# Who normalises the router's features, and in which order the vector engine works, in a fused graph and attention network

## The chip, the cores and the metric

The kernel runs on one core of a Trainium2 chip. The metric is the device time of one execution in microseconds (us), the median of several runs. Besides, one execution of the kernel is profiled, and everything below that is read from a trace is read from that one.

## The reference

Two layers, each with a graph part, a mixing part and a feed-forward part, over 1250 nodes of 512 values. What matters here is the end of the last layer: the graph part ends in a batch norm and a ReLU and is added to `x`; then `x` is layer-normalised and goes through a routed feed-forward net in which each of 32 experts takes its 39 best rows.

```python
h = h @ W2 + b2
h = jax.nn.relu(batch_norm(h, g2, be2))                 # end of the graph part
...
xf = _layernorm(x).reshape(bs, H)                       # (x - m) / sqrt(v + 1e-5), by row: the router's features
h = xf @ W_router + b_router
Sm = jax.nn.softmax(h, axis=-1)
G_ek, idx_ek = jax.lax.top_k(Sm.T, k)                   # 39 rows for each of 32 experts
tokens = xf[idx_ek]
up = jnp.einsum('gjkh,ghf->gjkf', tok_g, W_up) + b_up
act = jax.nn.silu(up)
Eout = jnp.einsum('ekf,efh->ekh', act, W_down) + b_down
y = zeros.at[idx_ek.reshape(-1)].add(G_ek * Eout)
x = x + y
```

## The kernel before, in words

The program is written for each engine by hand, with semaphores between them; every engine does its instructions in the order in which they stand. The 1250 rows are ten tiles of 125 rows (`TOK`), and the tiles form three groups (`GROUPS`): tiles 0 to 3, 4 to 7, and 8 and 9. The names that the change and the prediction's steps touch, in the order of the work:

- ScalarE applies batch norm and ReLU to the hidden values `H2T`, which lie with features on the partitions (L1050). TensorE turns them tile by tile with transposes (`gin_t`, L1606 to L1612, four transposes a tile) into one of two PSUM row banks, and the vector engine adds a tile from PSUM to `X` (L2211). `open_row` lets TensorE write a row bank only once the entry two before has been drained, so TensorE can be two tiles ahead of the vector engine at most.
- Layer norm of `X`: `stats` (L1717, L1720) takes mean and variance of the tiles of a group on the vector engine; GpSimd's `rstd` (L643, L645) makes 1/sqrt(variance + eps) of them with a power; `normalise` on the vector engine (L1725) writes `XF`, the router's features, and counts each tile on `ln_out`.
- `turn_rows("moe_t")` (L1137): TensorE waits until all ten tiles have been added to `X` (the row banks are then free), and for each group until its tiles of `XF` are there; it turns each group in four row entries, one for each 128 features, twelve entries in all. ScalarE drains each entry to `XFT` (`drain_turned`, L850).
- The gate: TensorE multiplies `XFT` with the router's weights (L1620), the vector engine adds the bias, a softmax follows (L2217 to L2225), and five rounds of top-8 search (L2235 to L2238) give the rows of each expert.
- SyncE stores `X` to the output and `XF` to DRAM (`xf_dram`, L458); GpSimd gathers the chosen rows from there (L804) once the search is done and both stores have landed. Then eight groups of four experts: products with `w_up` (L1676) and `w_down` (L1696), whose weights SyncE streams in from DRAM through a ring of buffers (L454), and a scatter into the output.
- `unread_products(n, entry)` (L1084 to L1088) is a helper on TensorE: n products of the identity with a constant, 256 columns wide, into a column bank of PSUM whose content nobody reads. It is used during the search and before the first gathered rows.

The order of the vector engine in the stretch around the change is this piece of code:

```python
for g, (lo, hi) in enumerate(GROUPS):
    for t in range(lo, hi):
        o = filled(ROW["gin_t"] + t)
        dve.tensor_tensor(X[:, t], o[0:TOK, :], X[:, t], ALU.add).then_inc(rows_free, 1)
    if g:
        normalise("moe", g - 1, X, XF)
    stats("moe", g, X, lambda t: dve.wait_ge(rows_free, ROW["gin_t"] + t + 1))
normalise("moe", 2, X, XF)
```

An earlier layer norm of the same kernel ("ffn") already has two of its groups normalised by ScalarE (L927), with a bias of -mean/std that GpSimd makes in two more instructions (L704, L705).

Of the kernel before, what the change touches and what calls it, by code (L numbers as in the profile page):

```python
# [5 lines left out]
ALU = mybir.AluOpType  # L6
ACT = mybir.ActivationFunctionType
# [16 lines left out]
GROUPS = [(0, 4), (4, 8), (8, 10)]  # L24
# [34 lines left out]
LN_EPS = 1e-5  # L59
# [99 lines left out]
def build(nc, a, out):  # L159
    with ExitStack() as ctx:  # L160
# [87 lines left out]
        X = rows(0)  # L248
# [367 lines left out]
        def _(pool):  # L616
# [29 lines left out]

            for g, (lo, hi) in enumerate(GROUPS):
# [49 lines left out]
            for g in range(2):  # L697
                lo, hi = GROUPS[g]
                rstd("sage", g)
                pool.wait_ge(ln_mv, LN_TILES["ffn", g])  # L700
                pool.tensor_scalar(ln_rs[:, lo:hi], ln_mv_t[:, lo:hi, 1], LN_EPS, None, ALU.add).then_inc(ln_eps, 1)
                pool.wait_ge(ln_eps, LN_NUMBER["ffn", g] + 1)
                done(pool.tensor_tensor(ln_rs[:, lo:hi], ln_rs[:, lo:hi], minus_half[:, lo:hi], ALU.pow))
                done(pool.tensor_tensor(ln_nm[:, lo:hi], ln_mv_t[:, lo:hi, 0], ln_rs[:, lo:hi], ALU.mult))  # L704
                pool.tensor_scalar(ln_nm[:, lo:hi], ln_nm[:, lo:hi], -1.0, None, ALU.mult).then_inc(ln_rstd, 1)  # L705
# [80 lines left out]
            for g in range(3):  # L786
                rstd("moe", g)
# [43 lines left out]
        def _(act):  # L831
# [8 lines left out]
            def drain_turned(stage, dst, affine=None):  # L840

                n = ROW[stage]
                for g, (lo, hi) in enumerate(GROUPS):
                    for c in range(C):
# [78 lines left out]
            def normalise_ffn(g):  # L923

                act.wait_ge(ln_rstd, LN_NUMBER["ffn", g] + 1)
                for t in range(*GROUPS[g]):
                    act.activation(XL[:, t], X[:, t], ACT.Identity, scale=ln_rs[:, t:t + 1],  # L927
                                   bias=ln_nm[:, t:t + 1]).then_inc(ln_out, 1)

# [13 lines left out]
            normalise_ffn(0)  # L943
# [4 lines left out]
            normalise_ffn(1)  # L948
# [102 lines left out]
            drain_turned("moe_t", XFT)  # L1051
# [19 lines left out]
        def _(pe):  # L1071
# [534 lines left out]
            for t in range(TILES):  # L1606
                if t in (0, 4, 8):
                    pe.wait_ge(bn2_relu, t + 4)
# [4 lines left out]

            turn_rows("moe_t", XF, "moe")
# [89 lines left out]
        def _(dve):  # L1704
# [503 lines left out]
            for g, (lo, hi) in enumerate(GROUPS):  # L2208
# [3 lines left out]
                if g:  # L2212
                    normalise("moe", g - 1, X, XF)
                stats("moe", g, X, lambda t: dve.wait_ge(rows_free, ROW["gin_t"] + t + 1))
            normalise("moe", 2, X, XF)
# [118 lines left out]
```

## Time and profile before

| | us |
|---|---|
| median of 3 runs | 1571.0 |
| lowest and highest run | 1566.73 and 1575.32 |
| the profiled execution, its time | 1569.41 |
| the profiled execution, its span (first to last instruction) | 1567.6 |

| engine | busy us | share of the span |
|---|---|---|
| TensorE matmul | 1431.1 | 91% |
| TensorE weight load | 957.2 | 61% |
| VectorE | 669.5 | 43% |
| GpSimd | 434.9 | 28% |
| ScalarE | 391.3 | 25% |

The span ends 1.8 us before the time does; both are of the same execution. The mean granted clock of TensorE is 0.969 of full speed. In the chain of work that ended last TensorE holds 78%, the vector engine 9% and DMA 7%. A share is an average over stages, so what one edit is worth is read in the stage that it touches, here the stretch from 1219 to 1244 us.

### The profile page before, as it was taken

Reading aid. Unit: us, or ns where it says so; the run is one execution under the profiler, and the core shown is the slowest. Engines: PE = TensorE matmul, PEld = TensorE weight load, DVE = VectorE, ACT = ScalarE, POOL = GpSimd, SP = SyncE. Lnnn points to the kernel's source line nnn. Section 1 sums busy time; section 2 is a strip of 40 time slices with the busy share of each in tenths; the row PEclk is TensorE's granted clock in tenths of the full one; section 3 lists DMA queues with packets and bytes.
Section 4 is the critical chain, followed back from the end, with each engine's and each line's share of the span. In section 5 each row is a group of like instructions: output and inputs, shape, how many; then the busy total and the mean of one; then the engine's idle time right before and its main releaser. Section 6 shows DMA issues by size and latency. Waiting matters only on the chain.

```text
span 1567.6 us, 18598 instructions
## 1 busy us (share of the span) xinstructions
PE 1431.1 (91%) x7122; PEld 957.2 (61%) x7122; DVE 669.5 (43%) x1252; ACT 391.3 (25%) x648; POOL 434.9 (28%) x432
## 2 busy tenths in 40 slices
PE   4999987999999799999999979999998689998996
PEld 2546744544777687666666635778866475554553
DVE  6522036789665424566666240624252651100100
ACT  2210002221412432544444324111151301000010
POOL 2300013002020310788888628002010112222111
PEclk9999998999999799999999999999999899999999
DMA  8000010031200230111110091012001949999995
GB/s 270 23 0 0 1 55 1 1 104 41 86 1 0 88 106 1 54 32 42 26 26 9 16 202 47 0 33 102 1 1 61 408 162 343 383 396 396 411 411 222
DMA packets 43789, 178.88 MB, mean 114 GB/s; under 512 B 6086, under 2 KB 6672, under 8 KB 41781
## 3 DMA queue, kind: packets, MB, share of 16 engines
q1 hardware_dynamic: 40141, 171.87, 30.7%
q0 software_dynamic: 3248, 5.48, 1.6%
q8 instruction: 57, 0.93, 0.2%
q10 hardware_dynamic: 313, 0.35, 0.1%
q14 instruction: 30, 0.25, 0.0%
HBM read 153.46 MB, written 21.66 MB: 112 GB/s over the span
## 4 chain that ended last, share of the span: by engine, by line
PE 78%; DVE 9%; DMA 7%; ACT 2%; issue 2%; POOL 1%; SPq 1%; DVEq 0%; POOLq 0%; ACTq 0%
PE psum L1696 9%; PE psum L1105 8%; PE psum L1096 7%; PE psum L1446 6%; PE psum L1676 5%; PE psum L1127 4%; PE psum L1432 3%; PE psum L1292 3%; PE psum L1537 3%; DMA arena<-in_w_down 3%; DMA arena<-in_w_in 3%; PE psum L1434 3%; PE psum L1246 2%; PE psum L1255 2%; PE psum L1310 2%; PE psum L1599 2%
## 5 line engine op out<-in xcount | busy, mean ns | idle before, releaser
L739 POOL TENSOR_TENSOR arena<-arena 125x420 f32<-125x420 f32 x192 | 178.3, 929 | 27.1
L1696 PE MATMUL psum<-arena 128*39 128x512 f32 (+1 forms) x704 | 157.4, 603 | 15.1 <-DMA arena<-in_w_down 8.8
L2044 DVE TENSOR_REDUCE neg_max<-psum 125x1 fp32r<-125x1250 f32 x80 | 116.8, 1460 | 100.9 <-PE psum L1400 53.2
L1004 ACT ACTIVATE arena<-psum 125x420 f32<-125x420 f32 x240 | 107.5, 521 | 124.1 <-PE psum L1434 124.1
L1696 PEld LDWEIGHTS psum<-arena 128*39 128x39 f32 (+1 forms) x704 | 51.7, 117 | 115.1 <-issue 108.2
L1096 PE MATMUL psum<-arena 128*128 128x512 f32 (+1 forms) x288 | 104.2, 523 | 6.1 <-DMA arena<-in_w_in 5.4
L824 POOL DMA_INDIRECT out_x<-arena,idx x32 | 44.9, 1402 | 209.4 <-DMA out_x<-arena,idx 118.3
L1446 PE MATMUL psum<-arena 125*64 125x210 f32 x960 | 102.7, 349 | 0.0
L1676 PEld LDWEIGHTS psum<-arena 128*128 128x128 f32 (+1 forms) x704 | 93.3, 187 | 8.0 <-issue 7.3
L1676 PE MATMUL psum<-arena 128*128 128x156 f32 (+1 forms) x704 | 95.4, 297 | 1.9 <-DMA arena<-in_w_up 1.4
L2269 DVE TENSOR_SCALAR arena<-psum,gates 39x512 f32<-39x512 f32 x32 | 24.0, 749 | 166.9 <-PE psum L1696 166.6
L1432 PE MATMUL psum<-arena_r 128*125 128x420 f32 x240 | 92.5, 386 | 0.7 <-ACT arena_r L993 0.7
L1096 PEld LDWEIGHTS psum<-arena 128*128 128x128 f32 x288 | 55.2, 193 | 55.0 <-issue 49.3
L1434 PE MATMUL psum<-arena_r 128*125 128x420 f32 (+1 forms) x240 | 84.9, 354 | 0.0
L1065 ACT ACTIVATE arena<-psum,vec 128x156 f32<-128x156 f32 (+1 forms) x88 | 28.2, 388 | 220.5 <-PE psum L1676 220.4
L1446 PEld LDWEIGHTS psum<-arena 125*64 125x64 f32 x960 | 61.9, 136 | 30.5 <-ACT arena L1004 16.0
L1865 DVE TENSOR_SCALAR arena<-arena,edge_key 125x500 bf16<-125x500 f16 x200 | 69.4, 347 | 25.0 <-PE psum L1230 23.9
L1127 PE MATMUL psum<-arena 128*125 128x512 f32 (+3 forms) x264 | 72.2, 433 | 1.7 <-ACT arena L873 1.3
L1137 PE MATMUL psum<-ident,arena 125*128 125x125 f32 x160 | 32.9, 356 | 34.7 <-DVE arena L1725 20.9
L671 POOL TENSOR_TENSOR arena<-arena 125x512 f32<-125x512 f32 x10 | 13.1, 1311 | 183.2 <-DVE arena L1847 183.2
L1127 PEld LDWEIGHTS psum<-arena 125*128 125x128 f32 (+2 forms) x264 | 43.4, 190 | 28.3 <-issue 23.2
L1432 PEld LDWEIGHTS psum<-arena_r 128*125 128x125 f32 x240 | 44.5, 186 | 24.7 <-issue 22.9
(407 smaller groups left out, 2451.7 us busy)
## 6 DMA issues: line engine op xcount, KB each, us to landing
arena<-in_w_down SPq DMA_DIRECT2D x96, 768.0 KB, 19.2
arena<-in_w_up SPq DMA_DIRECT2D x32, 682.5 KB, 19.4
arena<-in_w_down SPq DMA_DIRECT2D x32, 512.0 KB, 19.7
adj<-a_spill SPq DMA_DIRECT2D x1, 5468.8 KB
bc<-k_dram SPq DMA_DIRECT2D x16, 312.5 KB, 4.3
gw<-in_gw SPq DMA_DIRECT2D x2, 2048.0 KB, 9.3
arena<-in_wkqv SPq DMA_DIRECT2D x1, 3072.0 KB, 19.9
a_spill<-adj SPq DMA_DIRECT2D x1, 2843.8 KB
```

Of the source, the lines that this page charges most:

```text
L739: pool.tensor_tensor(SUMS[rnd % 2], SUMS[rnd % 2], PT[s % P_RING], ALU.add).then_inc(sum_added, 1)
L1004: act.activation(PT[s % P_RING], ring(step_entry(s))[:, 0:QW], ACT.Exp).then_inc(ring_done, 1)
L1096: ins = pe.matmul(o[0:w, lo:hi], lhs(c, m), rhs(c)[:, lo:hi], start=c == 0, stop=c == k - 1)
L1105: ins = pe.matmul(o[:, lo:hi], lhs[a_part][:, c, m * 128:m * 128 + 128], rhs[b_part][:, c, lo:hi], start=i == 0 and c == 0, stop=i == 2 an ...
L1127: ins = pe.matmul(o[0:p, 0:w], lhs(c, t), rhs(c, t), start=c == 0, stop=c == k - 1)
L1432: pe.matmul(o, KHH[h % 3][:, tok(t)], QS[:, h, q0:q1], start=True, stop=False)
L1434: pe.matmul(o, KLO[h % 2][rows_used, tok(t)], QM[h % 2][rows_used, q0:q1], start=False, stop=True).then_inc(ring_full, 1)
L1446: ins = pe.matmul(av_bank[rnd % 2][64 * i:64 * i + 64], VA[:, t, h * DK:h * DK + DK], PT[s % P_RING][:, i * QH:i * QH + QH], start=t == 0, ...
L1676: ins = pe.matmul(o[0:w, (f - 3 * q) * 512:(f - 3 * q) * 512 + 4 * CAP], UPQ[(4 * g + c) % 6][:, f * 128:f * 128 + w], TKT[g % 2][:, c], s ...
L1696: ins = pe.matmul(o[64 * j:64 * j + CAP, :], ACTT[g % 2][0:w, f, at:at + CAP], DN[e % 5][0:w, f], start=f == 0, stop=f == FT - 1)
L1865: dve.tensor_scalar(win_hot[s], win_iota, float(WIN_COLS * w), edge_key_all[:, bass.ds(tile, 1)], ALU.add, ALU.is_equal)
L2044: dve.tensor_reduce(neg_max[:, k:k + 1], max_bank[:, 0:N], AX.X, ALU.max, negate=True).then_inc(max_ready, 1)
```

## The change

Three things. The first group of `XF` is normalised by ScalarE (`normalise` in its block, called before it drains the first `moe_t` entry), and GpSimd makes the bias for it (`rstd_mean`, the code that "ffn" already used, now a function). The vector engine no longer normalises between its groups: it adds and takes the statistics of all three groups first and normalises groups 1 and 2 at the end. And TensorE gets four unread products before tile 4 of `gin_t` and six before `moe_t`.

```diff
+            def rstd_mean(name, g):
+
+                k, (lo, hi) = LN_NUMBER[name, g], GROUPS[g]
+                pool.wait_ge(ln_mv, LN_TILES[name, g])
+                pool.tensor_scalar(ln_rs[:, lo:hi], ln_mv_t[:, lo:hi, 1], LN_EPS, None, ALU.add).then_inc(ln_eps, 1)
+                pool.wait_ge(ln_eps, k + 1)
+                done(pool.tensor_tensor(ln_rs[:, lo:hi], ln_rs[:, lo:hi], minus_half[:, lo:hi], ALU.pow))
+                done(pool.tensor_tensor(ln_nm[:, lo:hi], ln_mv_t[:, lo:hi, 0], ln_rs[:, lo:hi], ALU.mult))
+                pool.tensor_scalar(ln_nm[:, lo:hi], ln_nm[:, lo:hi], -1.0, None, ALU.mult).then_inc(ln_rstd, 1)
...
-            for g in range(3):
-                rstd("moe", g)
+            rstd_mean("moe", 0)
+            rstd("moe", 1)
+            rstd("moe", 2)
...
-            def drain_turned(stage, dst, affine=None):
+            def normalise(name, g, src, dst):
+
+                act.wait_ge(ln_rstd, LN_NUMBER[name, g] + 1)
+                for t in range(*GROUPS[g]):
+                    act.activation(dst[:, t], src[:, t], ACT.Identity, scale=ln_rs[:, t:t + 1],
+                                   bias=ln_nm[:, t:t + 1]).then_inc(ln_out, 1)
+
+            def drain_turned(stage, dst, affine=None, ahead=None):
 
                 n = ROW[stage]
                 for g, (lo, hi) in enumerate(GROUPS):
+                    if ahead and g == 0:
+                        ahead(g)
...
-            drain_turned("moe_t", XFT)
+            drain_turned("moe_t", XFT, ahead=lambda g: normalise("moe", g, X, XF))
...
             for t in range(TILES):
                 if t in (0, 4, 8):
+                    if t == 4:
+                        unread_products(4, COL["up"])
                     pe.wait_ge(bn2_relu, t + 4)
...
+            unread_products(6, COL["up"])
             turn_rows("moe_t", XF, "moe")
...
                     dve.tensor_tensor(X[:, t], o[0:TOK, :], X[:, t], ALU.add).then_inc(rows_free, 1)
-                if g:
-                    normalise("moe", g - 1, X, XF)
                 stats("moe", g, X, lambda t: dve.wait_ge(rows_free, ROW["gin_t"] + t + 1))
+            dve.wait_ge(ln_out, LN_OUT["moe"] + GROUPS[0][1])
+            normalise("moe", 1, X, XF)
             normalise("moe", 2, X, XF)
```

The rest of the diff puts "ffn" on the same two functions, with the same instructions in the same order.

On the vector engine, from the first adds of the graph part to the gate, the order before (L2211 adds a tile, L1717 and L1720 are the statistics, L1725 normalises, L2217 is the gate's bias):

```order
L2211 TENSOR_TENSOR arena<-psum,arena 125x512 x4
L1717 BN_STATS ln_st<-arena 125x6 x4
L1720 BN_AGGR ln_mv_t<-ln_st 125x2 x4
L2211 TENSOR_TENSOR arena<-psum,arena 125x512 x4
L1725 TENSOR_SCALAR arena<-arena,ln_mv_t,ln_rs 125x512 x4
L1717 BN_STATS ln_st<-arena 125x6 x4
L1720 BN_AGGR ln_mv_t<-ln_st 125x2 x4
L2211 TENSOR_TENSOR arena<-psum,arena 125x512 x2
L1725 TENSOR_SCALAR arena<-arena,ln_mv_t,ln_rs 125x512 x4
L1717 BN_STATS ln_st<-arena 125x6 x2
L1720 BN_AGGR ln_mv_t<-ln_st 125x2 x2
L1725 TENSOR_SCALAR arena<-arena,ln_mv_t,ln_rs 125x512 x2
```

And in the changed kernel, where the same lines are ten further down:

```order
L2221 TENSOR_TENSOR arena<-psum,arena 125x512 x4
L1727 BN_STATS ln_st<-arena 125x6 x4
L1730 BN_AGGR ln_mv_t<-ln_st 125x2 x4
L2221 TENSOR_TENSOR arena<-psum,arena 125x512 x4
L1727 BN_STATS ln_st<-arena 125x6 x4
L1730 BN_AGGR ln_mv_t<-ln_st 125x2 x4
L2221 TENSOR_TENSOR arena<-psum,arena 125x512 x2
L1727 BN_STATS ln_st<-arena 125x6 x2
L1730 BN_AGGR ln_mv_t<-ln_st 125x2 x2
L1735 TENSOR_SCALAR arena<-arena,ln_mv_t,ln_rs 125x512 x6
```

Four of the ten normalising instructions have gone to ScalarE, and the six that are left stand behind the last add, which TensorE's `moe_t` waits for, instead of in front of it (four before stood ahead of that add).

On TensorE, the changed kernel between the last product of the graph part (L1587) and the gate (L1630); L1620 turns `gin_t`, L1144 turns `moe_t`, L1095 are the unread products:

```order
L1587 MATMUL psum<-k_sq,arena 125x512 x10
L1620 MATMUL psum<-ident,arena 125x128 x16
L1095 MATMUL psum<-neg_half,ident 128x256 x4
L1620 MATMUL psum<-ident,arena 125x128 x24
L1095 MATMUL psum<-neg_half,ident 128x256 x6
L1144 MATMUL psum<-ident,arena 128x125 x40
L1630 MATMUL psum<-arena,neg_half 32x315 x16
```

Before, the two rows of L1095 are not there, and the 40 transposes of `gin_t` stand in one piece.

## Rows read from the trace of the kernel before

**Rows 1.** The chain that ended last, 1190 to 1567 us: start us, us, what.

```profile
1219.94 0.72 PE psum L1611 x4
...
1222.85 2.38 DVE ln_st L1717 x4
1225.23 0.28 DVE ln_mv_t L1720 x4
1225.51 0.59 DVE arena L2211
...
1226.14 2.08 PE psum L1611 x8
...
1228.25 0.69 DVE arena L2211
1228.94 1.82 DVE arena L1725 x4
1230.76 2.38 DVE ln_st L1717 x4
1233.14 0.28 DVE ln_mv_t L1720 x4
1233.42 1.18 DVE arena L2211 x2
...
1241.39 0.60 ACT arena L850
...
1243.40 0.39 ACT arena L850
```

**Rows 2.** Busy time of each engine in stretches of the expert stage.

```profile
core 0: us, PE busy (x) PEld busy (x) DVE busy (x) ACT busy (x) POOL busy (x), PEclk, DMA share, GB/s
1283.00:1294.80 11.80, 11.80 (x90) 11.80 (x91) 0.00 (x0) 4.15 (x10) 1.54 (x2) 1.00 0.13 39
...
1310.00:1540.00 230.00, 213.84 (x1234) 127.63 (x1232) 24.72 (x38) 24.71 (x77) 45.79 (x35) 0.98 1.02 401
```

**Rows 3.** TensorE in order of time, 1219 to 1244 us.

```profile
1219.94 3.67 PE L1611 MATMUL psum<-ident,arena 128*125 128x128 f32 x20 [0.35 <-DVE arena L2181]
1226.14 3.81 PE L1611 MATMUL psum<-ident,arena 128*125 128x128 f32 x16 [2.53 <-DVE arena L2211]
1234.65 7.20 PE L1137 MATMUL psum<-ident,arena 125*128 125x125 f32 x34 [4.70 <-DVE arena L2211]
```

**Rows 4.** Busy time in single microseconds; columns as in the stretches above.

```profile
1225.00:1226.00 1.00, 0.00 (x0) 0.00 (x0) 1.00 (x7) 0.00 (x0) 0.32 (x2) 1.00 1.02 412
...
1228.00:1229.00 1.00, 0.98 (x5) 0.80 (x4) 0.84 (x3) 0.00 (x0) 0.00 (x0) 0.50 1.02 418
...
1230.00:1231.00 1.00, 0.00 (x0) 0.00 (x0) 1.00 (x3) 0.00 (x0) 0.00 (x0) 1.00 1.02 418
...
1236.00:1237.00 1.00, 1.00 (x6) 0.77 (x5) 1.00 (x3) 0.76 (x2) 0.00 (x0) 0.50 1.02 420
...
1240.00:1241.00 1.00, 0.97 (x8) 0.72 (x8) 0.37 (x1) 0.88 (x2) 0.00 (x0) 1.00 1.01 411
```

**Rows 5.** ScalarE in order of time, the drains of `moe_t`.

```profile
1235.78 0.59 ACT L850 ACTIVATE arena<-psum 128x500 f32<-128x500 f32 x1 [15.05 <-PE psum L1137]
1236.61 0.59 ACT L850 ACTIVATE arena<-psum 128x500 f32<-128x500 f32 x1 [0.24 <-PE psum L1137]
...
1239.38 2.88 ACT L850 ACTIVATE arena<-psum 128x500 f32<-128x500 f32 x5 [0.41 <-PE psum L1137]
```

**Rows 6.** ScalarE and GpSimd in order of time around 476 us, the "ffn" norm.

```profile
474.70 1.03 POOL L703 TENSOR_TENSOR ln_rs<-ln_rs,minus_half 125x4 f32<-125x4 f32 x1
...
476.38 2.94 ACT L927 ACTIVATE arena<-arena,ln_nm,ln_rs 125x512 f32<-125x512 f32 x4 [0.26 <-POOL ln_nm L705]
```

**Rows 7.** GpSimd in order of time, 1225 to 1235 us.

```profile
1225.91 1.04 POOL L645 TENSOR_TENSOR ln_rs<-ln_rs,minus_half 125x4 f32<-125x4 f32 x1
```

**Rows 8.** TensorE in order of time, one round of seven unread products (two records each).

```profile
1262.75 3.29 PE L1088 MATMUL psum<-neg_half,ident 128*128 128x256 f32 x14 [1.28 <-DVE arena L2238]
```

**Rows 9.** The vector engine in order of time, statistics of the last group.

```profile
1236.72 1.28 DVE L1717 BATCH_NORM_STATS2 ln_st<-arena 125x6 f32<-125x512 f32 x2
1237.92 0.30 DVE L1720 BATCH_NORM_AGGREGATE ln_mv_t<-ln_st 125x2 f32<-125x6 f32 x2
```

**Rows 10.** SyncE and GpSimd in order of time: next weights after the stores, first gather.

```profile
1266.09 1.30 SPq L454 DMA_DIRECT2D arena<-in_w_down  x3
1277.31 1.09 POOL L804 DMA_INDIRECT arena<-xf_dram,pair_idx  x1 [29.86 <-DVE pair_idx L2245]
```

More of the change, by code:

```diff
@@ L697, in _ @@
             for g in range(2):
-                lo, hi = GROUPS[g]
                 rstd("sage", g)
[L700 to L705, printed above, removed]
+                rstd_mean("ffn", g)
             rstd("sage", 2)
@@ L921, in high_sums @@
                 act.activation(AGG_PARTS[g][0][:, m, 0:w], agg_bank(k)[:, 0:w], ACT.Copy).then_inc(agg_hi, 1)
[L923 to L928, printed above, removed]
             def drain_ffn(g):
@@ L942, in _ @@
                 high_sums(1, m)
-            normalise_ffn(0)
+            normalise("ffn", 0, X, XL)
             high_sums(1, C - 1)
@@ L947, in _ @@
                 high_sums(2, m)
-            normalise_ffn(1)
+            normalise("ffn", 1, X, XL)
             drain_ffn(1)
```

## The prediction

> **What bounds the kernel now.** I first read the chain of work that ended last, because the change sits in a stretch of 25 us and only what lies on this chain counts. From 1222.85 us on the chain stays on the vector engine: statistics of group 0, adds, the four normalising instructions of group 0 (1.82 us), statistics of group 1 (2.38 and 0.28), and the two last adds (1.18), which end at 1234.60 [rows 1]. It leaves the engine only once, for 2.08 us, to wait for TensorE's turns of tiles 6 and 7. TensorE begins to turn the router's features at 1234.65, after 4.70 us without work [rows 3], and the last drain ends at 1243.40 + 0.39 = 1243.79 [rows 1].
>
> Next I read the expert stage, to see whether time saved here arrives at the end. Until 1294.8 TensorE does the first group's up products with hardly any DMA beside it (39 GB/s); from 1310 to 1540 the DMA share is 1.02 at 401 GB/s [rows 2]. So the end is set by a stream of weights that runs at the rate of the DMA engines. Most of it cannot start before the first group's up products have freed buffers, and those hang on the routing. A routing that ends x us earlier moves the start of the stream and with it the end by x.
>
> Last, the granted clock. It is 1.00 at 1225, 0.50 at 1228, 1.00 again at 1230, 0.50 at 1236 and 1.00 at 1240 [rows 4]: each fall to the half level (1.2 GHz) came after one of TensorE's two pauses, 2.53 and 4.70 us long [rows 3], each rise to 2.4 GHz came while or after TensorE turned tiles. These are the two waits that the change fills.
>
> **The change part by part.** 1. *Normalising group 0 leaves the vector engine's chain:* -1.82 us [rows 1].
>
> 2. *The same work on ScalarE.* GpSimd starts its power for group 0 at 1225.91 [rows 7]. In the "ffn" norm, which has the same instructions, ScalarE starts 476.38 - 474.70 = 1.68 us after the power's start and takes 2.94 us for four tiles [rows 6]. That gives 1225.91 + 1.68 + 2.94 = 1230.5 us. ScalarE has nothing else to do then: it sat idle for 15.05 us before its first drain [rows 5]. The features of group 0 are wanted when the last add is done, by the sum below at 1232.1, so the part is free with 1.6 us to spare. The two extra GpSimd instructions for the bias cost nothing either: the next group's statistics come some 5 us later. If that cover were gone, the cost would be what is left of the 2.94 us. Here a rule stands against the change. The trace has four tiles in 1.82 us on the vector engine and in 2.94 us on ScalarE [rows 1, 6]. The Trainium skill (ScalarE: Activation LUTs, Rules for kernel authors) says that multiplying and adding belong on VectorE and not on ScalarE. The trace agrees in kind, with 1.6 times for float32; by the rule alone the sum would be 1.1 us worse. I don't charge it, since the slower engine has the slack.
>
> 3. *Four unread products before tile 4.* Seven took 3.29 us at full clock [rows 8], 0.47 each, so four take 1.9. Tile 3's is the third of the turns that begin at 1219.94 [rows 3], so it ends near 1219.94 + 3 x 0.72 = 1222.1, the four end near 1224.0 and the turn of tile 4 (0.72 us for four transposes and the way to the vector engine, [rows 1]) near 1224.8. The vector engine asks for it at 1225.51 [rows 1]. Free, with 0.7 us to spare. TensorE's pause shrinks from 2.53 us to about 1.
>
> 4. *Tiles 6 and 7 turned at full clock.* Before, two turns cost 2.08 us at half clock, against 0.72 each [rows 1]. From 1226.14 the add of tile 6 starts at 1226.86 and that of tile 7 at 1227.58, where it started at 1228.25: -0.67 us. Bounds: 0 if the clock falls all the same, -0.67 if it does not. I take -0.67, as the pause that is left is far shorter than both after which the clock fell.
>
> With 1 and 4 the last add ends at 1234.60 - 1.82 - 0.67 = 1232.1.
>
> 5. *Six unread products before the features' turns:* 6 x 0.47 = 2.8 us. Tile 7's add ends at 1228.27 and frees the bank for tile 9, whose turn ends near 1229.0, so they end at 1231.8, before 1232.1. Free at full clock, but with only 0.3 us to spare; this is the tightest cover of the change. At half clock they take about 5.6 us, and then they stand in the way (rival 2).
>
> 6. *The late normalising of groups 1 and 2.* Four features' entries of group 0 are turned at once from 1232.1. Group 1 waits for the vector engine: statistics of group 2 take 1237.92 + 0.30 - 1236.72 = 1.50 us [rows 9], then normalising group 1 takes 1.82, so 1232.1 + 1.50 + 1.82 = 1235.4. This new wait takes the place of the old one. Group 0's four entries, drained at 2.88 / 5 = 0.58 us each [rows 5], are done at about the same time, so the loss by it is under 1 us. Group 2 follows about 1 us later, and is in time.
>
> 7. *The turns at full clock.* First drain of group 1 at 1235.4 + 0.72 = 1236.1 us, four drains at 0.60: 1238.5. From the end of group 1's last drain to the end of all took 1243.79 - (1241.39 + 0.60) = 1.80 us before, already at full clock [rows 1]. So the drains end at 1240.3, against 1243.79: **-3.5 us**. At half clock the drains came every 0.83 us [rows 5]. The bounds of this part are -1.8 (only the normalising goes) and -3.5. I take -3.4, near the far end, since rounding leaves 0.1.
>
> 8. *What comes after.* The gate, the softmax and the search keep their order and only start earlier. The stores: SyncE was held until the store of the features had landed and issued the next weights at 1266.09; the first gather started at 1277.31 [rows 10]. The gather waits for those stores too. With the routing 3.4 us earlier it starts at 1273.9, still 7.8 us behind the landing. So the gain passes.
>
> The profiled execution took 1569.41 us; the sum gives 1569.4 - 3.4 = 1566.0. It stands 1.6 us under the median of the runs shown, so on the median's scale the forecast is 1571.0 - 3.4 = **1567.6 us**, or -0.2%. That is below 0.5% (7.9 us), which is about what a measurement of this kernel can tell from no change.
>
> **The rivals.** *Rival 1, the clock falls all the same.* The products shorten the pauses but the half level still comes for one of the two stretches. For it: the level fell at about 1226.5, after TensorE had been busy until 1223.6 and had just begun again [rows 3, 4], so it lags what the engine does. Against it: the stretch from 1226 to 1232 is now nearly full. The result is -1.8, the normalising alone: 1569.2 us. The Trainium skill (TensorE: Matmul & The Clock Gate, What's actually happening) says that the number of slow matmuls at a start differs from run to run, which would make this rival come in some executions and not in others.
>
> *Rival 2, slower: the six products block the turns.* If the clock is at the half level when tile 9's turn ends, then near 1229.9 as before, the six end at 1229.9 + 5.6 = 1235.5, 0.9 us after TensorE starts on the features now. If the turns then run at the old pace, the result is +0.9: 1571.9 us. It decides from 0.79 us a product on ((1234.65 - 1229.9) / 6), against 0.47 at full clock. Against it: the clock had risen by 1230 even in the kernel before [rows 4].
>
> *Rival 3, the gain gets lost on the way.* The end is set by a stream of weights, and part of it is issued on the landing of the stores (1266.09), which does not move because the DMA engines are already full while `gin_t` and `moe_t` run (share 1.01 to 1.02, [rows 4]). If the first group's start hung on that, the result would be 1571.0 us, no change. Against it: 11 us between the landing and the gather [rows 10], and the DMA engines are nearly idle just before 1294.8 [rows 2].
>
> *Rival 4, more than forecast.* The stream of weights falls in a slightly better place. It lasts 230 us at 401 GB/s [rows 2]; 1% more rate is 2.3 us on top of the forecast: 1565.3 us. Nothing in the change makes it so.
>
> **How the numbers follow.** Forecast 0.55, rival 1 0.22, rival 2 0.07, rival 3 0.08, rival 4 0.08. All cases lie between 1565.3 and 1571.9. The three runs before lie up to 4.3 us from their median, and the median of the new ones may be off by a good part of that; so the range reaches some 3 us below the lowest case and 1.5 us above the highest: 1562.5 to 1573.5. Faster by over 0.5% means under 1563.1, which no case gives, only a case with the spread on top: 0.11. Slower by over 0.5% needs over 1578.9, 7 us above the worst case: 0.03. Within 0.5%: 0.86.
>
> **What the new profile would show.** ScalarE's four normalising instructions start near 1227.6 and end near 1230.5. TensorE's first feature turn starts near 1232.1, preceded by a pause under 1 us, and there is a short pause before group 1's turns, ended by the vector engine. The granted clock is 1.00 from 1219 to 1240 (rival 1: 0.50 somewhere in it; rival 2: 0.50 near 1230, and unread products that end after 1234). The last drain ends near 1240.3, the first gather starts near 1273.9, the next weights are issued near 1266 as now. The time from the first gather to the end stays as it is; if it grows by what the routing saved, rival 3 holds. I would be wrong if the vector engine waited for ScalarE's tiles, or if the turns waited for the unread products.

## The result and the profile after

| | before | after |
|---|---|---|
| median of 12 runs each, us | 1570.78 (1565.49 to 1575.32) | 1566.14 (1564.85 to 1569.07) |
| ratio | | 0.9975, interval 0.9963 to 0.9987 |
| profiled execution, us | 1569.41 | 1565.74 |
| its span, us | 1567.6 | 1563.8 |

The changed kernel is 3.9 us faster by the ratio (2.0 to 5.8 by its interval); the two medians themselves lie 4.6 us apart. The 3.9 us are a quarter of a per cent, inside the half per cent called "same" ahead of the result, and the 1566.1 us lie 1.5 us under the forecast of 1567.6.

The earlier stages do not start at the same microsecond in two traces, so everything below is counted from an **anchor**, the end of the last add of the graph part ahead of `gin_t` (1219.89 in the kernel before, 1218.88 in the changed one). The change's stretch ends with the last drain of `moe_t`: 23.90 us behind the anchor before (1243.79), now 1238.79 + 0.39 - 1218.88 = 20.30.

The chain that ended last, of the changed kernel (start us, us, what), answers to [rows 1]:

```profile
1221.85 2.38 DVE ln_st L1727 x4
1224.23 0.28 DVE ln_mv_t L1730 x4
1224.51 0.59 DVE arena L2221
...
1225.88 1.29 DVE arena L2221 x2
1227.17 2.38 DVE ln_st L1727 x4
1229.55 0.28 DVE ln_mv_t L1730 x4
1229.83 1.17 DVE arena L2221 x2
1231.00 1.19 DVE ln_st L1727 x2
...
1232.33 1.91 DVE arena L1735 x4
...
1234.29 0.66 PE psum L1144 x4
...
1238.79 0.39 ACT arena L864
```

Between the statistics of group 0 and those of group 1 the four normalising instructions are gone. They now stand behind the last add (1231.00), and the chain runs through them there: the new wait of the prediction's step 6.

ScalarE in order of time, of the changed kernel, answers to [rows 5, 6]:

```profile
1226.59 2.93 ACT L849 ACTIVATE arena<-arena,ln_nm,ln_rs 125x512 f32<-125x512 f32 x4 [8.55 <-POOL ln_nm L655]
```

The four tiles are ready at 1229.52. Nobody wants them before the last add, 1231.00, so 1.5 us are spare.

TensorE in order of time, of the changed kernel, answers to [rows 3]; the bracket is the idle time ahead of the group and what ended it:

```profile
1220.96 1.89 PE L1095 MATMUL psum<-neg_half,ident 128*128 128x256 f32 x8
...
1225.14 1.30 PE L1620 MATMUL psum<-ident,arena 128*125 128x128 f32 x8 [1.42 <-DVE arena L2221]
...
1227.77 2.76 PE L1095 MATMUL psum<-neg_half,ident 128*128 128x256 f32 x12
...
1231.06 1.07 PE L1144 MATMUL psum<-ident,arena 125*128 125x125 f32 x8 [0.54 <-DVE arena L2221]
...
1234.29 1.07 PE L1144 MATMUL psum<-ident,arena 125*128 125x125 f32 x8 [0.77 <-DVE arena L1735]
```

The pauses of 2.53 and 4.70 us have become 1.42, 0.54 and 0.77 us. An unread product has two records here and a transpose one, so `x8` is four products of L1095, but eight transposes. The whole stretch ran at the full level, as its busy times show (columns as in [rows 2]; the 1.00 behind the counts is the granted clock):

```profile
1216.00:1246.00 30.00, 21.38 (x141) 14.93 (x139) 20.25 (x44) 11.28 (x22) 5.33 (x11) 1.00 1.02 415
```

The span is 3.8 us shorter. In pieces: the stages ahead ended 2.7 us earlier, the piece just ahead of the anchor took 1.7 us more, the change's stretch 3.6 us less, the routing 0.3 us less, and the time from the first gather to the end 1.1 us more. Only the third of these five is the change's own; experiments had to say what the others are. The 0.3 us of the routing (last drain to first gather) come and go with the execution: it took 33.2 us in five of the fourteen traces below and 33.5 us in nine, and after_b, the changed kernel again, has 33.5.

### The profile page after: what moved, and what is told of

It reads as the page before. It is cut to its first block, busy times and chain, and to the rows that moved or that the text cites. A ratio compares the mean times of both kernels' runs of the same rounds, so it can differ in the third digit from the quotient of the medians.

```text
span 1563.8 us, 18641 instructions
## 1 busy us (share of the span) xinstructions
PE 1433.6 (92%) x7142; PEld 956.9 (61%) x7142; DVE 667.6 (43%) x1248; ACT 393.4 (25%) x652; POOL 436.5 (28%) x434
## 4 chain that ended last, share of the span: by engine, by line
PE 75%; DVE 9%; DMA 8%; SPq 3%; issue 2%; ACT 2%; POOL 1%; DVEq 0%; POOLq 0%; ACTq 0%
PE psum L1112 8%; PE psum L1706 7%; PE psum L1103 7%; PE psum L1453 6%; PE psum L1134 4%; DMA arena<-in_w_down 4%; PE psum L1686 4%; PE psum L1439 3%; PE psum L1299 3%; PE psum L1544 3%; DMA arena<-in_w_in 3%; PE psum L1441 3%; SPq L454 3%; PE psum L1253 2%; PE psum L1262 2%; PE psum L1317 2%
## 5 line engine op out<-in xcount | busy, mean ns | idle before, releaser
L1144 PE MATMUL psum<-ident,arena 125*128 125x125 f32 x160 | 28.9, 320 | 32.1 <-DVE arena L1735 22.0
```

## The experiments

There are five measures. **Ahead** is the time from ScalarE's last drain of `gin2`, the stage ahead, to the anchor. **Last add**, **first drain** and **last drain** are `gin_t`'s last add and `moe_t`'s drains, counted from the anchor. **Rest** runs from the first gather to the end. All in us, from one trace each.

| kernel | ahead | last add | first drain | last drain | rest |
|---|---|---|---|---|---|
| before | 11.07 | 14.71 | 15.9 | 23.90 | 290.3 |
| after | 12.77 | 12.12 | 12.86 | 20.30 | 291.4 |
| before_b | 14.08 | 14.18 | 15.38 | 22.83 | 291.3 |
| after_b | 11.07 | 12.13 | 12.87 | 20.29 | 293.4 |
| no_unread | 11.08 | 12.62 | 13.37 | 21.22 | 290.4 |
| unread_only | 11.07 | 13.94 | 14.68 | 21.80 | 292.0 |
| all_vector | 11.07 | 12.11 | 16.08 | 24.15 | 290.5 |
| twelve | 11.07 | 12.12 | 14.69 | 21.60 | 290.9 |
| double_scalar | 11.07 | 12.11 | 14.35 | 21.26 | 290.7 |
| down4_late | 14.04 | 12.12 | 12.85 | 20.27 | 290.7 |
| after_b2 | 14.09 | 12.11 | 12.85 | 20.28 | 291.1 |
| no_unread2 | 11.08 | 12.63 | 13.37 | 21.20 | 290.3 |
| best | 11.07 | 12.11 | 12.86 | 20.28 | 290.1 |
| g1_first | 14.08 | 12.12 | 12.86 | 20.05 | 290.9 |

All of them share one small edit in an early stage, so before_b is the kernel before with that edit, and after_b and after_b2 are the changed kernel with it. It adds a constant to both sides of a wait against a number, so that the number stays positive, and bounds the number where it is loaded:

```diff
-            done(dve.tensor_tensor(rng[:, 7], rng[:, 3], rng[:, 1], ALU.subtract))
+            done(dve.scalar_tensor_tensor(rng[:, 7], rng[:, 3], float(TILE_CODE // BODY), rng[:, 1], ALU.add, ALU.subtract))
...
-                dve.memset(small[0:1, 28 + s:29 + s], 0.0).then_inc(hot_free[s], BODY)
+                dve.memset(small[0:1, 28 + s:29 + s], 0.0).then_inc(hot_free[s], BODY + TILE_CODE)
...
-                turn = dve.value_load(ranges[0:1, 2 * WINDOWS + w:2 * WINDOWS + w + 1])
+                turn = dve.value_load(ranges[0:1, 2 * WINDOWS + w:2 * WINDOWS + w + 1], min_val=0, max_val=4 * TILE_CODE)
```

### The two kernels with that edit

> The kernel before, with one early edit that all my kernels share: the number that the vector engine waits against in the edge loop is kept positive (a constant 256 is added on both sides, one extra bound on the load). It touches nothing after 400 us. Measures, also for all later runs: A = from the end of the last drain of gin2 on ScalarE to the end of the last slice_o add; R = from there to the end of the last moe_t drain; G = from there to the first gather; S = from there to the end of the span. In the trace of before A is 11.1, R 23.9, G 33.5, S 290.3 us. Expected: the same within 0.3 us for R and G, 1566 to 1575 us in all. Rival: the edit costs time of its own: over 3 us more, all of it before 400 us.

Measured: 1573.36 us, ratio to before 1.0013 (0.9997 to 1.0029). The edit costs nothing that this can tell. The last drain came at 22.83, 1.1 us earlier than in the first trace of before, though nothing of this stretch was edited: the kernel before has a spread here of its own, since it depends on where the clock falls and rises. In the first trace 5.1 us of the `moe_t` turns ran at the half level (from 1234.65 to about 1239.7), in before_b 3.2 us (from 1237.85 to about 1241.0). Against the mean of the two, 23.4, the change is worth 3.1 us, not 3.6.

> The changed kernel with the same early edit. R was 20.3 us in the trace of after (R 3.6 shorter than before), A 12.8, G 33.2, S 291.4. Theory (the gain is made between the last slice add and the last drain, by 1.8 us of normalising off the vector engine's chain and the rest by a clock that stays at full level): R 20.3, time 3 to 5 us under before_b. Rival (a part of the gain of the medians is made elsewhere, or is spread of the runs): R 20.3 but under 2 us of difference in the times.

Measured: 1567.98 us, 0.9987 (0.9971 to 1.0003); last drain 20.29, the same as in the changed kernel to 0.01 us. The median lies 5.4 us under before_b's, where 3 to 5 us were expected, while against the kernel before the interval still includes no change; the times scatter by more than the stretch gives. The rest grew to 293.4 us, which is the subject of down4_late.

### Without the unread products, and the products alone

The edit of no_unread against the changed kernel; unread_only puts the same lines into the kernel before:

```diff
-                    if t == 4:
-                        unread_products(4, COL["up"])
...
-            unread_products(6, COL["up"])
```

> The changed kernel without its ten unread products; ScalarE's part and the new order stay. Theory (reordering and clock add up): the last add comes 1.8 us earlier than before, the clock falls to the half level in one of TensorE's waits, the drains come every 0.83 us: R 22.1, granted clock 0.50 in some microseconds between 1224 and 1240, time 1.5 to 2 us above after_b. Rival (the shorter waits of the new order keep the clock up without products): R 20.3 to 20.6, clock 1.00 throughout, time as after_b.

> The kernel before with the ten unread products alone; normalising and order as before. Theory: tiles 6 and 7 are turned at full clock (-0.67 us), the turns of moe_t begin 0.7 us earlier and run at full clock until group 2, which waits for the vector engine: R 22.4, time 1 to 2 us under before_b. Rival (the drains follow the clock alone, the vector engine is no limit): R 21.0. Second rival (the clock falls all the same, since the pause before moe_t is still 2 us): R 23.2 or more.

Without the products (no_unread) the last drain came at 21.22, not at about 22.1 as expected, and 1565.64 us, 0.9970 (0.9955 to 0.9985). With the products alone on the old order (unread_only) it came at 21.80, where 22.4 was expected, and 1569.37 us, 0.9986 (0.9971 to 1.0001). The times went other ways than expected: no_unread lay 2.3 us under after_b and not 1.5 to 2 us above it, and unread_only 4.0 us under before_b and not 1 to 2 us, so what follows is read from the traces. The new order, with ScalarE's part in it, is worth more, and the products less, than I had charged: on top of the new order the ten products save 21.2 - 20.3 = 0.9 us. On the old order they save between 1.0 us (22.83 - 21.80) and 2.1 us (23.90 - 21.80), depending on which trace of before one takes.

That the products do work through the clock is seen in TensorE's order of time without them, here from the repeat no_unread2:

```profile
1224.58 3.86 PE L1618 MATMUL psum<-ident,arena 128*125 128x128 f32 x16 [2.53 <-DVE arena L2218]
...
1231.01 4.71 PE L1144 MATMUL psum<-ident,arena 125*128 125x125 f32 x24 [2.57 <-DVE arena L2218]
```

and in its single microseconds:

```profile
1225.00:1226.00 1.00, 1.00 (x7) 1.00 (x6) 0.55 (x2) 0.00 (x0) 0.82 (x3) 0.50 1.06 434
...
1229.00:1230.00 1.00, 0.00 (x0) 0.00 (x0) 1.00 (x6) 0.00 (x0) 0.14 (x1) 1.00 1.06 436
...
1232.00:1233.00 1.00, 0.98 (x5) 0.67 (x4) 1.00 (x5) 0.86 (x2) 0.47 (x2) 0.50 1.02 405
```

The pauses of 2.53 and 2.57 us are each followed by a fall to 1.2 GHz. But the falls are short and cost 0.5 us at the last add (12.62 against 12.12) and 0.4 us behind it. The reason for the small price lies in the order itself: group 1 is not ready before the vector engine has normalised it, and slow turns of group 0 run in that wait. In the row above TensorE turns group 0 and half of group 1 in one piece of 24, where the changed kernel waits 0.77 us ahead of group 1.

In unread_only the pause ahead of `moe_t` is still 2.36 us:

```profile
1233.56 1.07 PE L1137 MATMUL psum<-ident,arena 125*128 125x125 f32 x8 [2.36 <-DVE arena L2214]
```

Eight transposes in 1.07 us is the pace at the full level, the same as in the changed kernel. A pause of that length did not bring the half level here.

### ScalarE's part taken back

```diff
-            rstd_mean("moe", 0)
+            rstd("moe", 0)
...
-            drain_turned("moe_t", XFT, ahead=lambda g: normalise("moe", g, X, XF))
+            drain_turned("moe_t", XFT)
...
-            dve.wait_ge(ln_out, LN_OUT["moe"] + GROUPS[0][1])
+            normalise("moe", 0, X, XF)
```

> The changed kernel, but group 0 is normalised by the vector engine too, behind the last add (GpSimd then makes no bias for it). Theory: the last add is where it was (12.1 us after the last slice add), and the turns of moe_t wait for group 0, ready at 12.1 + 1.5 (statistics of group 2) + 1.8 = 15.4, so the first drain starts at 16.1, the rest follows at 0.58 us an entry and R is 22.7, against 20.3. So ScalarE's part is worth 2.4 us once the order is changed. Rival (ScalarE's part only frees the engine of 1.8 us): R 22.1. Rival (the order alone is the change): R 20.5.

A single run, 1570.32 us beside 1570.07 for before; last drain 24.15, where 22.7 was expected and the changed kernel has 20.3. TensorE in order of time of all_vector:

```profile
1235.77 1.04 PE L1144 MATMUL psum<-ident,arena 125*128 125x125 f32 x8 [3.79 <-DVE arena L1735]
...
1237.06 5.41 PE L1144 MATMUL psum<-ident,arena 125*128 125x125 f32 x26 [0.25 <-ACT arena L864]
```

All ten normalising instructions now stand behind the last add, and TensorE waits 3.79 us for the first four. Then the clock falls to the half level (0.50 at 1238) and the rest of the turns runs slowly: that second part I had left out of the expectation. The whole gain is gone, so moving the normalising to ScalarE carries the change. The new order without it is no better than the old one. What ScalarE's part would give on the old order was not run.

### How much cover there is

One kernel has twelve products in place of six ahead of the turns; the other makes ScalarE normalise group 0 twice.

```diff
-            unread_products(6, COL["up"])
+            unread_products(12, COL["up"])
```

> The changed kernel with twelve unread products before moe_t where it has six. Six take 2.8 us and end 0.5 us before they would be in the way. Theory (they have little cover): the twelve end at about 14.4 us after the last slice add, where the turns now begin at 12.2; the first drain moves from 12.9 to 15.1, and since group 0's four entries then delay group 1 from 15.4 to about 17.0, R is 22.0. Rival (the turns wait for the vector engine's group 1 anyway, and the cover is that long): R 20.3 to 20.8.

```diff
+                if name == "moe":
+                    for t in range(*GROUPS[g]):
+                        act.activation(dst[:, t], src[:, t], ACT.Identity, scale=ln_rs[:, t:t + 1],
+                                       bias=ln_nm[:, t:t + 1]).then_inc(ident_ready, 1)
+                    act.wait_ge(ident_ready, 5)
```

> The changed kernel, where ScalarE normalises group 0 twice (the second pass counts), so that its part takes 5.9 us instead of 2.9. It measures the slack: ScalarE's four tiles were ready 1.5 us before TensorE wanted them. Theory: the turns begin 1.4 us later, at 13.6 instead of 12.2 after the last slice add, group 1 follows at about 16.3 instead of 15.4, R 21.2. Rival (group 1 is the wait that counts, and it hides the delay): R 20.3 to 20.5. Rival (no slack: the vector engine, which waits for these tiles before it normalises group 1, passes on all of it): R 23.2.

With twelve (a single run, 1567.02 us) the products take 5.35 us, TensorE begins the turns as soon as they end, and the first drain comes 1.8 us later (14.69 against 12.86):

```profile
1227.24 5.35 PE L1095 MATMUL psum<-neg_half,ident 128*128 128x256 f32 x24
...
1232.42 1.02 PE L1144 MATMUL psum<-ident,arena 125*128 125x125 f32 x8
```

Six more products are 5.35 - 2.76 = 2.59 us, and they cost 1.3 us at the last drain (21.60, where 22.0 was expected). The idle 0.54 us behind the six is the cover of step 5, and of the 1.8 us that the first drain is late, group 1's own wait absorbs another 0.5. With double_scalar (a single run, 1566.56 us) ScalarE makes a second pass behind the first:

```profile
1229.58 2.93 ACT L854 ACTIVATE arena<-arena,ln_nm,ln_rs 125x512 f32<-125x512 f32 x4
```

TensorE's first turn comes at 1232.61 after 2.06 us without work, and the last drain at 21.26, where 21.2 was expected. So 2.93 us more on ScalarE cost 1.5 us at the first drain (14.35 against 12.86): 1.4 to 1.5 us of it were spare. The cover of step 2 is measured.

### The gain behind the routing

In after_b the rest took 293.4 us, where the other thirteen traces have 290.1 to 292.0. SyncE, GpSimd and TensorE in order of time, of after_b:

```profile
1266.05 2.05 SPq L454 DMA_DIRECT2D arena<-in_w_down  x4
...
1272.82 1.09 POOL L809 DMA_INDIRECT arena<-xf_dram,pair_idx  x1 [29.88 <-DVE pair_idx L2255]
...
1277.67 0.49 PE L1669 MATMUL psum<-ident,arena 78*128 78x78 f32 x4 [1.85 <-DMA arena<-xf_dram,pair_idx]
```

and two of its single microseconds, the DMA share being the last column but one:

```profile
1272.00:1273.00 1.00, 1.00 (x6) 0.90 (x5) 0.23 (x2) 0.00 (x0) 0.18 (x1) 1.00 1.01 416
...
1274.00:1275.00 1.00, 1.00 (x6) 0.88 (x5) 0.00 (x0) 0.00 (x0) 0.78 (x1) 1.00 0.79 287
```

The weights that SyncE issues once the stores have landed keep the DMA engines busy until some 8.6 us behind their issue. The first gather was issued 6.8 us behind it, into the end of that load, and TensorE waited 1.85 us for its rows. In the changed kernel's first trace the two stood 9.3 us apart and did not meet:

```profile
1263.10 1.99 SPq L454 DMA_DIRECT2D arena<-in_w_down  x4
...
1272.40 1.09 POOL L809 DMA_INDIRECT arena<-xf_dram,pair_idx  x1 [29.57 <-DVE pair_idx L2255]
```

An overlap by itself does no harm, though. In five more traces the gather was issued before the end of the load, 7.8 to 8.6 us behind its issue, and TensorE waited 0.20 to 0.30 us, as where the two are well apart. The nearest is no_unread2, at 7.8 us:

```profile
1265.26 2.02 SPq L454 DMA_DIRECT2D arena<-in_w_down  x4
...
1273.05 1.09 POOL L809 DMA_INDIRECT arena<-xf_dram,pair_idx  x1 [29.87 <-DVE pair_idx L2252]
...
1276.25 0.49 PE L1666 MATMUL psum<-ident,arena 78*128 78x78 f32 x4 [0.20 <-DMA arena<-xf_dram,pair_idx]
```

Between issue and rows there is time for the load to end: in the changed kernel the DMA engines are nearly idle from 1273 to 1274 (share 0.01), after the issue at 1272.40, and at 0.51 in the next microsecond.

The next kernel lets this load wait until the first gathered blocks have been turned:

```diff
-            sp.wait_ge(rows_full, ROW["moe_t"] + 12)
+            sp.wait_ge(rows_full, TOKEN_ROW[1] + 1)
```

> The changed kernel, but SyncE loads the fifth expert's weights (2.8 MB, about 8 us of all DMA engines) only when the first two gathered blocks have been turned, and not when the stores have landed. In the trace of after_b these weights ran from 1267 to 1275 us, the first gather was issued at 1272.8 into them, and TensorE waited 1.85 us for it where it waits 0.3 in the other five traces. Theory (the earlier routing now runs into this load in some executions, which takes back up to 1.5 us): TensorE's wait for the first gather is 0.3 us in this profile, first gather to first turn 3.3 us, and the times are 0.5 to 1.5 us under after_b's 1568.0. Rival (the late load is missed later, in the second group): TensorE waits for weights of group 1, and the span from gather to end grows by 3 us or more. Rival (nothing): as after_b.

> after_b once more, beside the next three. It tells how much of a difference between two kernels' medians is the kernel: after_b and no_unread had medians of 1568.0 and 1565.6 although no_unread's R is 0.9 us longer. Theory (executions differ by the clock in an earlier wait, A 11.1 or 12.8 to 14, and by how the first gather meets the fifth expert's weights; neither is of this change): R 20.3 again, the median anywhere from 1565 to 1569. Rival (the ten products cost something further on): median again 2 us or more above no_unread2's.

Measured for down4_late: 1566.45 us, 0.9982 (0.9964 to 1.0); for after_b2: 1568.28 us, 0.9978 (0.9957 to 0.9999). TensorE's wait for the first gathered rows is short in down4_late:

```profile
1283.77 0.49 PE L1669 MATMUL psum<-ident,arena 78*128 78x78 f32 x4 [0.17 <-DMA arena<-xf_dram,pair_idx]
```

and the rest is 290.7 us, so nobody misses the load when it comes later. But the repeat of the changed kernel, with the load in its old place, has 291.1. The collision is in one of three traces of the whole change with the load in its old place, and in one of twelve traces of all kernels with it there. The late load takes away its possibility; the runs' times do not show a gain by it, and as no second collision was seen, that it costs the 2 us rests on one trace. Against the kernel before, the changed kernel has now stood at 0.9975, 0.9987 and 0.9978, that is 3.9, 2.0 and 3.5 us, and the interval of the second includes no change.

> no_unread once more on the same chip as after_b2. Theory: R 21.0 to 22.1 (the clock falls somewhere in the two waits), median within 1.5 us of after_b2's, with the sign open. Rival (the products are of harm): 2 us or more under after_b2.

Measured: 1568.58 us, 0.9997 (0.9982 to 1.0012), last drain 21.20. In the trace it repeats no_unread to 0.02 us; in time it lies 2.9 us above it, and level with after_b2 on the same chip (1568.28), while beside after_b the kernel without products had been 2.3 us better than the one with them. The products' 0.9 us are beyond what these times can tell.

### A third wait, and the two edits together

The piece ahead of the anchor took 11.07 us in some traces and 14.1 in others. It holds a wait of 2.83 us for the vector engine, in front of the second group of the graph part's last product. TensorE in order of time, of before_b:

```profile
1214.47 8.42 PE L1580 MATMUL psum<-k_sq,arena 128*125 128x512 f32 x12 [2.83 <-DVE arena L2181]
```

A microsecond behind the wait, in the same kernel, at the half level:

```profile
1216.00:1217.00 1.00, 1.00 (x2) 0.33 (x1) 0.00 (x0) 1.00 (x3) 0.00 (x0) 0.50 1.04 436
```

The changed kernel's own trace has the same wait, with 7.11 us for the same twelve products and the half level for a shorter time:

```profile
1211.04 7.11 PE L1587 MATMUL psum<-k_sq,arena 128*125 128x512 f32 x12 [2.83 <-DVE arena L2191]
```

In the thirteen traces without products in this wait the clock fell in five (12.77 us in one, 14.0 to 14.1 in four) and not in eight. When it fell it cost 1.7 to 3.0 us, 1.05 on average over the thirteen. This accounts for the 1.7 us that the changed kernel's span lost ahead of the anchor; the change had no part in it, since the traces of both kernels have both values. The kernel best is down4_late with five products in this wait as well:

```diff
+                if t == SLICE_FIRST + 2:
+                    unread_products(5, COL["up"])
```

> The changed kernel with two more edits: five unread products in TensorE's wait of 2.83 us before the eighth slice_o tile (the wait for batch norm), and the fifth expert's weights loaded only when the first gathered blocks have been turned. Theory: A is 11.1 us and cannot become 12.8 to 14.1, R 20.3, gather without a queue before it; the median is 1 to 2 us under after_b2's and the highest times come down. Rival (the products are late for the eighth tile): A 11.4 or more in every execution. Rival (the clock in that wait is not what lengthens A): A 12.8 or more in this profile and the times as after_b2's.

Its trace shows the products, the wait of 0.67 us that is left, and the same twelve products in 5.42 us:

```profile
1205.63 2.32 PE L1095 MATMUL psum<-neg_half,ident 128*128 128x256 f32 x10
...
1208.63 5.42 PE L1587 MATMUL psum<-k_sq,arena 128*125 128x512 f32 x12 [0.67 <-DVE arena L2193]
```

Measured: 1564.9 us, 0.9970 (0.9955 to 0.9986) against before, the lowest of all, with 11.07 ahead of the anchor and 290.1 behind the gather. It beats the kernel before. Its median lies 3.4 us under that of the changed kernel with the same early edit (after_b2), where 1 to 2 us were expected; but with a scatter of 10 to 13 us in each, that it beats this one too is not shown. One trace at 11.07 is what eight of thirteen have without the edit.

### Group 1 normalised before the last group's statistics

```diff
+                if g == 2:
+                    dve.wait_ge(ln_out, LN_OUT["moe"] + GROUPS[0][1])
+                    normalise("moe", 1, X, XF)
                 stats("moe", g, X, lambda t: dve.wait_ge(rows_free, ROW["gin_t"] + t + 1))
-            dve.wait_ge(ln_out, LN_OUT["moe"] + GROUPS[0][1])
-            normalise("moe", 1, X, XF)
```

> The changed kernel, where the vector engine normalises group 1 before the statistics of group 2 and not after. Theory (the one wait left among the turns, 0.77 us for group 1, moves to group 2): group 1 follows group 0 with no wait, group 2's tiles are ready at about 17.8 us after the last slice add, 0.6 later than wanted, R 20.0 to 20.1. Rival (group 2 was in time with room to spare): R 19.5. Rival (GpSimd's power for group 1 holds the vector engine): R 20.3 or more.

A single run, 1565.61 us, last drain 20.05, as expected. The wait ahead of group 1 has gone and one ahead of group 2 has come:

```profile
1237.38 0.65 PE L1144 MATMUL psum<-ident,arena 125*128 125x125 f32 x4 [0.68 <-DVE arena L1735]
```

This order is worth a quarter of a microsecond. The new wait of step 6 was a small loss, as forecast.

## Why the prediction was right, and where it was not

In the stretch of the change the steps came as described, and their sum did too; what was mis-sized is how it divides between the order and the clock. That the profiled execution, 1565.74 us, lies so close to the sum's 1566.0 is in part luck: the pieces outside the sum (2.7 us less, 1.7 and 1.1 us more) happened to cancel.

All figures are counted from the anchor, so that the drift of the earlier stages does not enter.

- **Steps 1 and 4**, the last add: forecast 12.2, measured 12.12. The tiles 6 and 7 were turned at the full level (1.30 us for two, [rows 1] has 2.08).
- **Step 2**, ScalarE ready: forecast 10.6, measured 10.6, spare 1.5 us where 1.6 was forecast; double_scalar confirmed it. The four instructions took 2.93 us, as the "ffn" norm's did [rows 6], against 1.91 us for four on the vector engine at the new place. So the rule of the Trainium skill (ScalarE: Activation LUTs, Rules for kernel authors) holds in kind, and it did not decide: all_vector, which follows it, ends 3.9 us later.
- **Steps 3 and 5**, the products: 1.9 and 2.8 us forecast, 1.89 and 2.76 measured; 0.3 us spare forecast, 0.54 measured. Rival 2 did not come; twelve products show what it would have looked like.
- **Step 6**, group 1 ready: forecast 15.5, measured 15.35. The wait was 0.77 us.
- **Step 7**, the drains' end: forecast 20.4, measured 20.30, that is 3.6 us earlier than in the trace of before, where 3.5 was forecast. The 20.3 came out the same in all five traces of kernels with the whole change (20.27 to 20.30).

Four points need mending although the sum came out.

- **The size against the one trace of before.** [Rows 3, 4] show one of two ways in which the old kernel runs: before_b had 22.83 where it had 23.90. The gain on an average execution is nearer 3.1 us. The bound of step 7 at the far end (-3.5) was that of a bad execution.
- **The readings of the clock.** The prediction has each fall come after a pause. In the trace of before the second one came inside it: TensorE was idle from 1229.95 to 1234.65, and the half level stands in the microsecond from 1233, behind 0.95 in the one from 1232:

```profile
1233.00:1234.00 1.00, 0.00 (x0) 0.00 (x0) 1.00 (x7) 0.00 (x0) 0.41 (x2) 0.50 1.05 418
```

The first fall, put at about 1226.5, was at about 1226.1 (the clock of the microsecond from 1226 is 0.54), when TensorE was just beginning again. In before_b the clock fell near 1230.8 and stayed at the half level through the whole second pause. In step 6, the 0.58 us a drain is from a row of five of which one is narrow (128x250, 0.38 us); the wide ones take 0.59, which changes nothing.
- **The share of the clock.** Steps 4 and 7 gave 1.6 us of the 3.5 to the clock, and the products were to bring it. Of that, products on the new order bring 0.9 us. The new order without any product already has a second pause of 2.57 us in place of 4.70, and what a slow turn loses is partly hidden by the wait for group 1. I had computed one sum for both parts and not the case of one without the other.
- **Step 8, "so the gain passes".** The argument stopped at the landing of the stores, 7.8 us ahead of the forecast gather. Behind the landing stands the load of weights that SyncE then issues. In [rows 10] it is issued at 1266.09, and the DMA engines are busy with it until about 1274.7, so the forecast gather at 1273.9 is issued into its end. no_unread2 shows that 7.8 us is still free (0.20 us of waiting, a rest of 290.3 us). after_b, at 6.8 us, met the load, in one trace: its rows came 1.5 us late and the rest was 2.0 us longer than in the changed kernel's trace. What the step left out is that the landing itself moves: SyncE issued the load 3 us earlier in the changed kernel's trace, which put 9.3 us between the two. So rival 3 came true in one trace, in part and by another mechanism than the one I gave it.

The piece ahead of the anchor was in no step. I had looked for pauses only where the diff adds products; the pause of 2.83 us ends 10 us ahead of the first of them, and is longer than the 2.53 us one that I argued from. In the trace of before it did not lower the clock, which hid it.

What stays open: why the same 2.83 us lower the clock in one execution and not in the next; why the rest took 292.0 us in unread_only and 291.4 in the changed kernel, where no collision was seen; and where the earlier stages' spread comes from. In fourteen traces the end of the stage ahead lies between 1203.7 and 1213.1 us, by far the largest share of a run's scatter, and it owes nothing to this change. The 2.7 us that the changed kernel's trace gained there are such scatter, and they covered the 1.7 us of the third wait and the 1.1 us of the rest.

## What to carry to other kernels

Work on the engine whose chain everybody waits for is cheapest on a slower engine that is idle. Compare the moment when its result is ready with the moment when it is asked for, not the two engines' durations. Ahead of moving a reader of DRAM earlier, look at what the DMA engines do at its new time, up to the end of the last load that is issued there and not only to the event that both wait for, and at how far that load moves between executions. And when a price depends on the clock, take it from two traces at least, and cost each part of the change also without the others.

## What was unexpected in the hardware

**The same pause, two outcomes.** A wait of 2.83 us in one place was followed by the half level (1.2 GHz) in five of thirteen traces and not in eight, with the same work ahead of it. Pauses of 2.53 to 2.59 us lowered it in both traces without products, one of 2.36 us did not. The Trainium skill (TensorE: Matmul & The Clock Gate, What's actually happening) speaks of a number of slow matmuls at a kernel's start that differs between runs. The traces agree, in the middle of a kernel, with 0, 1.7 or 3.0 us lost at one spot.

**GpSimd slows beside the vector engine's normalising.** GpSimd's power for the last group now runs while the vector engine normalises group 1. GpSimd in order of time, of the changed kernel:

```profile
1232.50 0.45 POOL L643 TENSOR_SCALAR ln_rs<-ln_mv_t 125x2 f32<-125x2 f32 x1 [1.24 <-DVE ln_mv_t L1730]
1233.03 0.86 POOL L645 TENSOR_TENSOR ln_rs<-ln_rs,minus_half 125x2 f32<-125x2 f32 x1
```

In the kernel before the same two took 0.23 and 0.71 us, beside an idle vector engine. The Trainium skill (SBUF — State Buffer, Who interferes with whom) tells of a port pair that these two engines share and lock; the trace agrees with 0.22 and 0.15 us more for each, though no run here tested it apart. It costs nothing, as group 2 is ready in time.

**SyncE is held in the issue of its own store.** SyncE issues the store of `X` in two instructions, and the second took 11.93 us in the changed kernel, probably since weights that were issued ahead of it filled the queue (argued, not tested):

```profile
1231.42 11.93 SPq L458 DMA_DIRECT2D out_x<-arena  x1
```

How long it is held differs between executions (the two took 8.2 to 14.1 us together over the fourteen traces), and with it the time at which the next weights are issued (1263.10 in the changed kernel, 1266.05 in after_b). The distance to the gather, 9.3 us in the one and 6.8 us in the other, moves with it.
